# Attention: one reduce instruction for the row maxima of both heads of a pair

## The chip, the core and the metric

The kernel runs on one core of one Trainium2 chip. The metric is the device time of one execution in microseconds, as a median over several. The engines are named as in the profile: PE (TensorE, with its weight loads as PEld), DVE (VectorE), ACT (ScalarE), POOL (GpSimd) and SP (SyncE, here the issuer of DMAs).

## What is computed

Input x has 2 sequences of 2048 tokens with 256 features. Layer 0 adds a state-space scan and a product with sign weights. Layer 1 adds two attentions, each followed by its output product, and a mixture of 8 experts (top 2). The change lies in the two attentions alone:

```python
scores = einsum('bhqd,bhkd->bhqk', Q, K) * scale      # 16 heads of 16 features, causal
attn   = softmax(scores, axis=-1)                     # row maximum, exp, sum
out    = einsum('bhqk,bhkd->bqhd', attn, V)
```

The first has 16 heads of keys and values and position slopes added to the scores; the second has 4 heads of keys and values shared by 4 query heads each. The softmax subtracts each row's maximum, so the maxima of all rows over their causal keys are needed before the exponentials.

## The kernel before

The attention stage runs 16 steps (`STEPS`): 2 attentions, 2 sequences, 4 groups of 4 heads. The heads of a group are taken in pairs, `p` = 0 and 1; the two heads `j` = 0, 1 of a pair lie in the lower and the upper half of the partitions, so that PE can work at both at once. Query rows are cut into 4 blocks of 512 (`QB`).

Scores are made twice in a step. First come the maxima: for 128 queries and up to 512 keys (`WIDE`), PE writes queries x keys of both heads into two banks of PSUM (L1271, `max_pair` of the PE part, L1264), and on the diagonal adds masks with small bf16 products (L1256). DVE reduces each bank over its columns (L1444, `max_pair` of the DVE part, L1437) into `mx`. When all pieces of a block are there, L1451 reduces `mx` over the pieces, POOL splits the result into a high and a low part (L1215, L1217), PE turns it into rows (L1298), ACT copies them (L1394), and SP stores them by DMA as two more operand rows of the queries (L1163). Second come the scores proper, keys x queries, with these rows subtracting the maxima (L1286, `score_pair`), again two banks a pair; ACT takes the exponentials of each bank into `prob` (L1404), and PE multiplies the values with it, four heads side by side, into bank 7 (L1367). ACT copies a finished block out (L1424), PE turns it (L1376), and DVE divides by the row sums (L1465, L1469).

A step has 80 maxima pairs (`NMX`), 80 score pairs (`NSP`), 40 value products, 4 "rows" and 4 "turn" items. Their order is written out as a string (`ORDER`, and `FIRST_ORDER` for the first step, which has 130 maxima pairs since maxima run 50 pairs ahead, `LEAD`). All engines walk through the same list, each in order.

Banks 0 to 6 form a ring (`RING` = 7). `slot_table` (L1002) deals slots in the order of the list: two for a maxima or score pair, one for "rows" and "turn". A pair with slot number u sits in banks u mod 7 and (u + 1) mod 7, so it can wrap from bank 6 to bank 0. Before PE writes slots u and u + 1 it waits in `free_slots` (L1301) until slots u - 7 and u - 6 are free: for each kind of work it finds the newest item held there and waits once for its count. For maxima the semaphore is `s_md`, and each single reduce adds one to it, so there are 160 counts a step. For scores it is `s_ex`, one count for each exponential.

Of the kernel before, what the change touches and what calls it, by code (L numbers as in the profile page):

```python
# [6 lines left out]
ALU = mybir.AluOpType  # L7
ACT = mybir.ActivationFunctionType
AX = mybir.AxisListType
# [920 lines left out]
NQB = L // QB  # L930
KT = L // P
WIDE = 512
RING = 7
# [23 lines left out]
NSP, NMX = len(SCORES), len(MAXES)  # L957
# [44 lines left out]
def slot_table(work):  # L1002

    at, held = {}, []
    for what, n in work:
        if what in ("max", "score"):
            at[what, n] = len(held)
            held += [(what, 2 * n), (what, 2 * n + 1)]
        elif what in ("turn", "rows"):
            at[what, n] = len(held)  # L1010
            held.append((what, n))
    return at, held


def attention(nc, A, M):
# [4 lines left out]
    with ExitStack() as ctx:  # L1020
        def sb(name, shape, dt=F32):
            return ctx.enter_context(nc.sbuf_tensor(name, shape, dt))

        def sem(name):
            return nc.alloc_semaphore(name)

        ps, ident = M["ps"], M["ident"]
# [5 lines left out]
        mx = sb("a_mx", [P, 2, PAIRS, KT, L // WIDE])  # L1033
# [15 lines left out]
        s_md = sem("att_max_tile_reduced")  # L1049
# [21 lines left out]
        NSC = 2 * NSP  # L1071
        EX0, PV0, OE0, TT0, TE0, RT0, RE0, MP0, TOP0, MD0, HI0 = 16, NPB // GH, 1, 2, NQB, 1, NQB, 1, NQB, 512, 2
# [7 lines left out]
        def slot_sem(t):  # L1080

            return t if t < 2 else 2 + (t - 2) % 3
# [162 lines left out]
        def _(pe):  # L1245
# [55 lines left out]
            def free_slots(t, held, first, count):  # L1301

                last = {}
                for u in range(first - RING, first - RING + count):
                    past = u < 0
                    if past and t == 0:
                        continue
                    before = FIRST_HELD if t == 1 else HELD
                    what, n = before[u] if past else held[u]
                    while what == "pad":  # L1310
                        u -= RING
                        what, n = before[u]
                    back = {"max": 2 * NMX, "score": NSC, "turn": NQB, "rows": NQB}[what] if past else 0
                    last[what] = max(last.get(what, -1000), n + 1 - back)
                if "max" in last:
                    pe.wait_ge(s_md, t * (2 * NMX) + (last["max"] + MD0))
                if "turn" in last:
                    pe.wait_ge(s_te, t * NQB + (last["turn"] + TE0))
                if "rows" in last:
                    pe.wait_ge(s_re, t * NQB + (last["rows"] + RE0))  # L1320
                if "score" in last:
                    pe.wait_ge(s_ex, t * NSC + (last["score"] + EX0))

            pe.wait_ge(s_q[0], NFIRST)
            def step(t):
                o = t % 3
                work = work_of(t)
                slot_of, held = slot_table(work)
                for what, n in work:
                    if what != "value":  # L1330
                        u = slot_of[what, n]
                        outs = [ps[(u + j) % RING] for j in range(2)]
                    if what == "rows" and t == 0 and n == 0:
                        keep_going(pe, M, ps_o, 10)
                    if what == "max":
                        if t == 0 and n == KEYED[0]:
                            pe.wait_ge(s_k[0], NFK)
                        if t == 0 and n == KEYED[1]:
                            pe.wait_ge(s_k[1], NFK)
                        if n == NMX:  # L1340

                            pe.wait_ge(s_q[slot_sem(t + 1)], filled(t + 1) * NL)
                        free_slots(t, held, u, 2)
                        max_pair(t + n // NMX, n, outs)
                    elif what == "rows":
                        free_slots(t, held, u, 1)
                        turn_rows(t, n, u % RING)
                    elif what == "score":
                        qb, kt, p = SCORES[n % NSP]
                        if kt == 0 and p == 0:  # L1350

                            pe.wait_ge(s_mr[qb], (t + n // NSP + 1) * NMR)
                        free_slots(t, held, u, 2)
                        score_pair(t + n // NSP, n, outs)
                    elif what == "value":
                        qb, kt, _ = SCORES[n * PAIRS]
                        c0 = columns(qb, kt)
                        if n == 0:
                            pe.wait_ge(s_v[slot_sem(t)], filled(t) * 16)
                        if kt == 0:  # L1360

                            pe.wait_ge(s_oe, t * NQB + (qb + OE0))

                        pe.wait_ge(s_ex, t * NSC + (n * GH + GH + EX0))
                        for h in range(GH):
                            hk = 0 if t >= NGB else h
                            ins = pe.matmul(ps_o[VW * h:VW * h + VW, c0:QB], v_op[o][:, kt, hk * VW:hk * VW + VW],  # L1367
                                            prob[:, (n * GH + h) % NPB, c0:QB], start=(kt == 0),
                                            stop=(kt == 4 * qb + 3))
                        ins.then_inc(s_pv, 1)  # L1370
                    else:

                        free_slots(t, held, u, 1)
                        pe.wait_ge(s_oe, t * NQB + (n + 1 + OE0))
                        for j in range(4):
                            ins = pe.transpose(outs[0][:, j * P:(j + 1) * P],  # L1376
                                               o_sb[n % 2][:, j * P:(j + 1) * P], ident[:, :])
                        ins.then_inc(s_tt, 1)
# [50 lines left out]
        @block.vector  # L1429
        def _(dve):  # L1430
            v = nc.vector
            ch = Chain(dve, s_dve)
            dve.sem_inc(s_te, TE0)
            dve.sem_inc(s_md, MD0)
            dve.sem_inc(s_top, TOP0)

            def max_pair(t, n, banks):  # L1437
                qb, p, qt, k0, w = MAXES[n % NMX]
                if n % NMX == 0 or MAXES[n % NMX - 1][0] != qb:

                    dve.wait_ge(s_top, t * NQB + (n // NMX * NQB + qb - NQB + 1 + TOP0))
                dve.wait_ge(s_mt, t * NMX + (n + 1))
                for j in range(2):
                    v.tensor_reduce(mx[:, j, p, qt, k0 // WIDE:k0 // WIDE + 1], ps[banks[j]][:, 0:w], AX.X,  # L1444
                                    ALU.max).then_inc(s_md, 1)
                if n % NMX == LAST_MAX[qb]:
                    block = n // NMX * NQB + qb

                    dve.wait_ge(s_mp, t * NQB + (block + MP0))
                    dve.wait_ge(s_md, t * (2 * NMX) + (2 * (n + 1) + MD0))  # L1450
                    v.tensor_reduce(row_top[:, :, :], mx[:, :, :, 4 * qb:4 * (qb + 1), 0:qb + 1].rearrange(  # L1451
                        "p j h k c -> p (j h) k c"), AX.X, ALU.max).then_inc(s_top, 1)

            def step(t):
                work = work_of(t)
                slot_of = slot_table(work)[0]
                for what, n in work:
                    if what == "max":
                        max_pair(t, n, [(slot_of[what, n] + j) % RING for j in range(2)])
                    elif what == "turn":  # L1460
                        turned = ps[slot_of[what, n] % RING].rearrange("p (j h c) -> p j h c", j=4, h=GH)
                        dve.wait_ge(s_te, t * NQB + (n + TE0))
                        dve.wait_ge(s_tt, t * NQB + (n + 1 + TT0))

                        ch.did(v.reciprocal(rec[:, :, :], turned[:, :, :, HD]))  # L1465
                        ch.settle()

                        dve.wait_ge(s_os[n % 2], t * (NQB // 2 * 16) + (n // 2 * 16 + 16))
                        v.tensor_tensor(o_row[n % 2][:, :, :].rearrange("p j (h c) -> p j h c", h=GH),  # L1469
                                        turned[:, :, :, 0:HD],  # L1470
                                        rec[:, :, :].unsqueeze(3).to_broadcast([P, 4, GH, HD]), ALU.mult
                                        ).then_inc(s_te, 1)

            for t in range(STEPS):
                step(t)
# [884 lines left out]
```

## Time and profile before

| | us |
|---|---|
| median of 3 runs (lowest, highest) | 2559.83 (2559.28, 2562.41) |
| span of the profiled execution, first to last instruction | 2553.9 |
| its own time: the span and what lies around it, by the median | 2559.83 - 2553.9 = 5.9 around the span |
| attention stage in the profiled execution | 369.6 to 1972.3 |
| DVE busy, whole span | 1919.1 (75%) |
| PE busy, whole span | 2345.1 (92%) |
| L1444, the reduces | x2560, 1378.0 busy |

Busy is the time in which an engine had at least one instruction under way; instructions on one engine overlap a little, so the sum of their durations is more than the busy time. The idle time before an instruction is put down to the event that ended it. The mean granted clock of TensorE is given beside a stretch, 1.00 being 2.4 GHz.

### The profile page before, as it was taken

What the parts mean: (1) busy time and instruction counts of PE and PEld (TensorE: products, weight loads), DVE (VectorE), ACT (ScalarE), POOL (GpSimd) and SP (SyncE); (2) the same over time, 40 slices, a digit from 0 to 9 for tenths busy, and PEclk for the clock granted to TensorE, in tenths of its full rate; (3) what the DMA queues carried; (4) which work ended last, traced back from release to release, by engine and by line L of the source; (5) the groups of instructions that cost most, each with busy time, mean ns of one, the idle gap of its engine ahead of it and who ended that gap; (6) DMA issues with size and microseconds to landing.
All of it is one profiled execution on the core that took longest, in us unless ns stands there. A gap on an engine that the chain in (4) does not pass through costs nothing. (4 is left out here: it accounts for less than half of the span.)

```text
span 2553.9 us, 53242 instructions
## 1 busy us (share of the span) xinstructions
PE 2345.1 (92%) x18418; PEld 1285.1 (50%) x18419; DVE 1919.1 (75%) x4030; ACT 1519.8 (60%) x3292; POOL 583.1 (23%) x845
## 2 busy tenths in 40 slices
PE   3599988999999999999999999999999873999997
PEld 2355554444444444444444444444443662788886
DVE  7777659999999998998998999999992573333332
ACT  2133314777778778777787787777778561222221
POOL 5412002121111111111111111111000266432223
PEclk8799997999999999999999999999999996999999
DMA  4267775453343443322322322322121894344443
GB/s 157 77 194 217 209 182 91 72 110 76 67 85 76 71 79 70 62 51 54 63 56 46 71 54 48 66 54 52 31 79 37 290 299 173 68 75 76 77 74 70
DMA packets 168303, 246.56 MB, mean 97 GB/s; under 512 B 52392, under 2 KB 125240, under 8 KB 162244
## 3 DMA queue, kind: packets, MB, share of 16 engines
q0 software_dynamic: 38304, 112.51, 23.8%
q1 hardware_dynamic: 124740, 120.83, 16.1%
q10 hardware_dynamic: 5044, 10.32, 1.3%
q8 instruction: 139, 2.28, 0.4%
q14 instruction: 76, 0.62, 0.1%
HBM read 120.19 MB, written 122.36 MB: 95 GB/s over the span
## 5 line engine op out<-in xcount | busy, mean ns | idle before, releaser
L1444 DVE TENSOR_REDUCE a_mx<-banks 128x1 f32<-128x512 f32 (+3 forms) x2560 | 1378.0, 602 | 127.6 <-PE banks L1271 60.1
L1404 ACT ACTIVATE a_p<-banks 128x512 f32<-128x512 f32 (+3 forms) x2560 | 1177.9, 541 | 332.7 <-PE banks L1286 202.2
L1367 PE MATMUL banks<-a_p,a_v 128*32 128x512 f32 (+3 forms) x5120 | 599.3, 543 | 0.9 <-ACT a_p L1404 0.5
L1271 PE MATMUL banks<-a_k,a_q 48*128 48x512 f32 (+7 forms) x1600 | 340.7, 429 | 9.7 <-ACT a_p L1404 2.6
L1286 PE MATMUL banks<-a_q,a_k 50*128 50x512 f32 (+7 forms) x1600 | 332.2, 426 | 11.6 <-DVE a_mx L1444 4.4
L1271 PEld LDWEIGHTS banks<-a_k,a_q 52*128 52x128 f32 (+1 forms) x1600 | 154.6, 184 | 207.2 <-DVE a_mx L1444 164.5
L1286 PEld LDWEIGHTS banks<-a_q,a_k 54*128 54x128 f32 (+1 forms) x1600 | 152.3, 184 | 201.1 <-DVE a_mx L1444 145.3
L2136 ACT ACTIVATE e_hT<-banks 128x256 fp32r<-128x256 f32 x72 | 27.6, 383 | 308.7 <-PE banks L2062 279.0
L1271 PE MATMUL banks<-a_k,q 48*128 48x512 f32 (+7 forms) x896 | 192.0, 433 | 8.5 <-DMA a_k<-aug_rows 2.6
L2075 PE MATMUL banks<-w,e_hT 128*128 x576 | 184.1, 421 | 12.5 <-DVE e_hT L2176 11.6
L1286 PE MATMUL banks<-q,a_k 50*128 50x512 f32 (+7 forms) x896 | 186.8, 429 | 6.9 <-ACT a_p L1404 2.9
L2176 DVE TENSOR_TENSOR e_hT<-banks,e_hT 128x256 fp32r<-128x256 f32 x72 | 30.6, 424 | 192.7 <-ACT e_hT L2136 192.7
L2042 POOL DMA_INDIRECT out_rows<-e_y,e_token x72 | 111.6, 1550 | 250.9 <-DVE e_y L2196 173.1
L1367 PEld LDWEIGHTS banks<-a_p,a_v 128*32 128x32 f32 x5120 | 102.9, 108 | 113.8 <-issue 62.8
L1271 PEld LDWEIGHTS banks<-a_k,q 48*128 48x128 f32 (+1 forms) x896 | 87.8, 187 | 117.0 <-DVE a_mx L1444 91.6
L1286 PEld LDWEIGHTS banks<-q,a_k 50*128 50x128 f32 (+1 forms) x896 | 84.8, 185 | 122.9 <-DVE a_mx L1444 77.4
L2094 PE MATMUL banks<-w,e_gT 128*128 x576 | 136.5, 380 | 1.5 <-DVE e_y L2196 1.1
L2075 PEld LDWEIGHTS banks<-w,e_hT 128*128 128x128 f32 x576 | 109.6, 191 | 37.2 <-issue 13.8
L1256 PE MATMUL banks<-fill,before 64*128 64x64 bf16 x2048 | 124.6, 198 | 0.0
L1256 PE MATMUL banks<-fill,after 64*128 64x64 bf16 x2048 | 121.4, 197 | 0.0
L2094 PEld LDWEIGHTS banks<-w,e_gT 128*128 128x128 f32 x576 | 103.8, 190 | 13.5 <-issue 2.3
L1206 POOL DMA_DIRECT2D expert_rows<-a_zeros x132 | 98.6, 747 | 3.2 <-issue 3.2
(267 smaller groups left out, 2551.2 us busy)
## 6 DMA issues: line engine op xcount, KB each, us to landing
expert_rows<-a_zeros POOLq DMA_DIRECT2D x132, 258.0 KB, 5.4
a_k<-ka_parts POOLq DMA_DIRECT2D x42, 256.0 KB, 6.4
e_x<-expert_rows SPq DMA_DIRECT2D x72, 129.0 KB, 2.9
expert_rows<-e_y SPq DMA_DIRECT2D x72, 128.0 KB, 2.2
qa_parts<-m_part SPq DMA_DIRECT2D x16, 512.0 KB, 4.4
ka_parts<-m_part SPq DMA_DIRECT2D x16, 512.0 KB, 4.7
va_tiles<-m_va SPq DMA_DIRECT2D x8, 1024.0 KB, 4.5
qb_parts<-m_part SPq DMA_DIRECT2D x16, 512.0 KB, 4.8
```

The costliest lines, as they stand in the source:

```text
L1206: pool.dma_start(hs[:, i * FILL:(i + 1) * FILL, :], zeros[:, :, :]).then_inc(s_zs, 16)
L1256: ins = pe.matmul(outs[j][:, HALF * n:HALF * (n + 1)], steps[n][half, :], fill[half, :], start=False, stop=(n == 1))
L1271: ins = pe.matmul(outs[j][:, 0:w], q_op[o][part, p, qt * P:(qt + 1) * P], keys_of(r, k0)[part, kp, k0:k0 + w], start=True, stop=not diagonal)
L1286: ins = pe.matmul(outs[j][:, c0:QB], keys_of(r, kt * P)[part, kp, kt * P:(kt + 1) * P], q_op[o][part, p, qb * QB + c0:(qb + 1) * QB], star ...
L1367: ins = pe.matmul(ps_o[VW * h:VW * h + VW, c0:QB], v_op[o][:, kt, hk * VW:hk * VW + VW], prob[:, (n * GH + h) % NPB, c0:QB], start=(kt == ...
L1404: nc.scalar.activation(prob[:, (2 * n + j) % NPB, c0:QB], ps[(slot + j) % RING][:, c0:QB], ACT.Exp, scale=SCALE).then_inc(s_ex, 1)
L1444: v.tensor_reduce(mx[:, j, p, qt, k0 // WIDE:k0 // WIDE + 1], ps[banks[j]][:, 0:w], AX.X, ALU.max).then_inc(s_md, 1)
L2042: pool.indirect_dma_start(out=out, out_offset=bass.IndirectOffsetOnAxis(ap=token[n % R][:, :], axis=0), in_=y[n % R][:, :], in_offset=None ...
L2075: ins = pe.matmul(bank[:, :], hT[c][s][:, k, :], of[:, ds(at, 1), part * FFN:(part + 1) * FFN].rearrange("p o m -> p (o m)"), start=(k == ...
L2094: ins = pe.matmul(ps_y[:, 0:D], gT[s][:, f, :], w2[:, ds(e * FT + f, 1), :].rearrange("p o m -> p (o m)"), start=(f == 0), stop=(f == FT - 1))
L2136: nc.scalar.activation(hT[0][s][:, :, :].rearrange("p k t -> p (k t)"), ps_h[:, 0:D], ACT.Copy).then_inc(s_hi, 1)
L2176: v.tensor_tensor(hT[1][s][:, :, :].rearrange("p k t -> p (k t)"), ps_h[:, 0:D], high, ALU.subtract).then_inc(s_hT, 1)
```

## The change

Where the two banks of a maxima pair are neighbours, DVE reduces them with one instruction that reads both banks (2 x w columns) and writes two maxima. Where the pair wraps from bank 6 to bank 0, two instructions stay, and the banks are taken in the order 0, 6 by PE and by DVE. The semaphore `s_md` is raised once a pair, behind the last instruction of the pair, and `slot_table` counts both slots of a maxima pair under the pair's own number, so PE waits for whole pairs. The order strings are the same.

```diff
--- before.py
+++ after.py
@@ -1003,13 +1003,21 @@
 
     at, held = {}, []
     for what, n in work:
-        if what in ("max", "score"):
+        if what == "max":
+            at[what, n] = len(held)
+            held += [(what, n), (what, n)]
+        elif what == "score":
             at[what, n] = len(held)
             held += [(what, 2 * n), (what, 2 * n + 1)]
         elif what in ("turn", "rows"):
             at[what, n] = len(held)
             held.append((what, n))
     return at, held
+
+
+def pair_slots(u):
+
+    return sorted(((u + j) % RING for j in range(2)))
 
 
 def attention(nc, A, M):
@@ -1310,10 +1318,10 @@
                     while what == "pad":
                         u -= RING
                         what, n = before[u]
-                    back = {"max": 2 * NMX, "score": NSC, "turn": NQB, "rows": NQB}[what] if past else 0
+                    back = {"max": NMX, "score": NSC, "turn": NQB, "rows": NQB}[what] if past else 0
                     last[what] = max(last.get(what, -1000), n + 1 - back)
                 if "max" in last:
-                    pe.wait_ge(s_md, t * (2 * NMX) + (last["max"] + MD0))
+                    pe.wait_ge(s_md, t * NMX + (last["max"] + MD0))
                 if "turn" in last:
                     pe.wait_ge(s_te, t * NQB + (last["turn"] + TE0))
                 if "rows" in last:
@@ -1333,6 +1341,7 @@
                     if what == "rows" and t == 0 and n == 0:
                         keep_going(pe, M, ps_o, 10)
                     if what == "max":
+                        outs = [ps[slot] for slot in pair_slots(u)]
                         if t == 0 and n == KEYED[0]:
                             pe.wait_ge(s_k[0], NFK)
                         if t == 0 and n == KEYED[1]:
@@ -1434,20 +1443,25 @@
             dve.sem_inc(s_md, MD0)
             dve.sem_inc(s_top, TOP0)
 
-            def max_pair(t, n, banks):
+            def max_pair(t, n, slots):
                 qb, p, qt, k0, w = MAXES[n % NMX]
                 if n % NMX == 0 or MAXES[n % NMX - 1][0] != qb:
 
                     dve.wait_ge(s_top, t * NQB + (n // NMX * NQB + qb - NQB + 1 + TOP0))
                 dve.wait_ge(s_mt, t * NMX + (n + 1))
-                for j in range(2):
-                    v.tensor_reduce(mx[:, j, p, qt, k0 // WIDE:k0 // WIDE + 1], ps[banks[j]][:, 0:w], AX.X,
-                                    ALU.max).then_inc(s_md, 1)
+                low, high = slots
+                if high == low + 1:
+                    ins = v.tensor_reduce(mx[:, :, p, qt, k0 // WIDE], M["banks"][:, low:high + 1, 0:w], AX.X, ALU.max)
+                else:
+                    for j in range(2):
+                        ins = v.tensor_reduce(mx[:, j, p, qt, k0 // WIDE:k0 // WIDE + 1], ps[slots[j]][:, 0:w], AX.X,
+                                              ALU.max)
+                ins.then_inc(s_md, 1)
                 if n % NMX == LAST_MAX[qb]:
                     block = n // NMX * NQB + qb
 
                     dve.wait_ge(s_mp, t * NQB + (block + MP0))
-                    dve.wait_ge(s_md, t * (2 * NMX) + (2 * (n + 1) + MD0))
+                    dve.wait_ge(s_md, t * NMX + (n + 1 + MD0))
                     v.tensor_reduce(row_top[:, :, :], mx[:, :, :, 4 * qb:4 * (qb + 1), 0:qb + 1].rearrange(
                         "p j h k c -> p (j h) k c"), AX.X, ALU.max).then_inc(s_top, 1)
 
@@ -1456,7 +1470,7 @@
                 slot_of = slot_table(work)[0]
                 for what, n in work:
                     if what == "max":
-                        max_pair(t, n, [(slot_of[what, n] + j) % RING for j in range(2)])
+                        max_pair(t, n, pair_slots(slot_of[what, n]))
                     elif what == "turn":
                         turned = ps[slot_of[what, n] % RING].rearrange("p (j h c) -> p j h c", j=4, h=GH)
                         dve.wait_ge(s_te, t * NQB + (n + TE0))
```

## Rows read from the trace of the kernel before

**Rows 1.** The page: span; busy us, share and instructions of each engine

```profile
span 2553.9 us, 53242 instructions
PE 2345.1 (92%) x18418; PEld 1285.1 (50%) x18419; DVE 1919.1 (75%) x4030; ACT 1519.8 (60%) x3292; POOL 583.1 (23%) x845
```

**Rows 2.** Windows: first step, 14 equal steps, last step; busy us (instructions), clock

```profile
core 0: us, PE busy (x) PEld busy (x) DVE busy (x) ACT busy (x) POOL busy (x), PEclk, DMA share, GB/s
369.60:522.40 152.80, 138.40 (x1188) 66.56 (x1188) 138.98 (x273) 85.25 (x181) 30.68 (x63) 0.89 0.53 88
522.40:1893.00 1370.60, 1341.39 (x12993) 613.09 (x12992) 1249.83 (x2409) 1083.45 (x2352) 231.26 (x449) 1.00 0.33 63
1893.00:1972.30 79.30, 76.12 (x691) 30.14 (x690) 36.64 (x69) 69.72 (x158) 4.02 (x8) 1.00 0.24 68
```

**Rows 3.** Waits, eleven steps 717.7 to 1795.3: us, times, longest

```profile
PEld banks L1271 <- DVE a_mx L1444: 181.9, 384, 0.8
...
PEld banks L1286 <- DVE a_mx L1444: 159.7, 281, 1.1
...
DVE a_mx L1444 <- PE banks L1271: 41.0, 113, 0.9
DVE a_mx L1444 <- PE banks L1256: 36.0, 98, 0.7
```

**Rows 4.** Timeline, two places: start us, us, instruction, idle before and releaser

```profile
750.77 0.69 DVE L1444 TENSOR_REDUCE a_mx<-banks 128x1 f32<-128x512 f32 x1
...
751.38 0.68 DVE L1444 TENSOR_REDUCE a_mx<-banks 128x1 f32<-128x512 f32 x1
751.52 0.18 PEld L1286 LDWEIGHTS banks<-q,a_k 54*128 54x128 f32 x2 [0.24 <-DVE a_mx L1444]
...
1790.94 1.29 DVE L1444 TENSOR_REDUCE a_mx<-banks 128x1 f32<-128x512 f32 x2
...
1791.68 0.18 PEld L1286 LDWEIGHTS banks<-a_q,a_k 50*128 50x128 f32 x2 [0.18 <-DVE a_mx L1444]
```

**Rows 5.** Lines by form, DVE, one step 913.3 to 1011.3: count, busy us, mean ns

```profile
L1444 DVE TENSOR_REDUCE a_mx<-banks 128x1 f32<-128x512 f32 x112 | 70.3, 683 | 5.4 <-PE banks L1271 3.8 <-PE banks L1256 1.0
L1444 DVE TENSOR_REDUCE a_mx<-banks 128x1 f32<-128x384 f32 x16 | 8.1, 548 | 0.7 <-PE banks L1256 0.7
L1444 DVE TENSOR_REDUCE a_mx<-banks 128x1 f32<-128x256 f32 x16 | 6.0, 417 | 0.3 <-PE banks L1256 0.2
L1444 DVE TENSOR_REDUCE a_mx<-banks 128x1 f32<-128x128 f32 x16 | 3.9, 283 | 1.2 <-PE banks L1256 1.2
...
L1451 DVE TENSOR_REDUCE a_rowtop<-a_mx 128x16 f32<-128x64 f32 x1 | 0.2, 219 | 0.1
```

**Rows 6.** Timeline of DVE: two heads of one pair, back to back

```profile
1008.47 1.28 DVE L1444 TENSOR_REDUCE a_mx<-banks 128x1 f32<-128x512 f32 x2
```

**Rows 7.** Timeline: a burst on DVE, and a maxima pair behind a value product on PE

```profile
723.34 13.14 DVE L1444 TENSOR_REDUCE a_mx<-banks 128x1 f32<-128x512 f32 x23
...
730.89 1.07 PE L1367 MATMUL banks<-a_p,a_v 128*32 128x512 f32 x8
...
731.89 0.49 PE L1271 MATMUL banks<-a_k,q 52*128 52x512 f32 x2
```

**Rows 8.** The page: the chain that ended last, by line

```profile
PE banks L2075 7%; PE banks L2094 5%; PE banks L2086 1%; PE banks L2062 1%; DMA out_rows<-e_y,e_token 0%; DMA e_last<-expert_rows,places 0%; DMA expert_rows<-e_y 0%; POOL t_w13low L2028 0%; DVE e_y L2196 0%; SPq L1995 0%; DVE e_sum L2221 0%; DVE e_sum L2223 0%; POOLq L1951 0%; DVE e_hT L2176 0%; POOL e_last L2035 0%
```

**Rows 9.** Timeline, two places where PE started before its pair was reduced

```profile
720.45 0.28 DVE L1444 TENSOR_REDUCE a_mx<-banks 128x1 f32<-128x128 f32 x1
...
720.47 0.38 PEld L1286 LDWEIGHTS banks<-q,a_k 54*128 54x128 f32 x4 [0.18 <-issue]
...
1792.45 1.28 DVE L1444 TENSOR_REDUCE a_mx<-banks 128x1 f32<-128x512 f32 x2
...
1793.45 0.19 PEld L1286 LDWEIGHTS banks<-a_q,a_k 50*128 50x128 f32 x2
```

## The prediction

> **What bounds the kernel now.** I read the busy shares first, then the stretches, then the waits, then single microseconds of the timeline. The attention stage runs from 369.6 to 1972.3 us, 1602.7 of the 2553.9 us [rows 1, 2]. Its 16 steps are one pattern: a long first step, 14 equal ones of 97.9 us (1370.6 / 14), and a short last one with hardly a maximum in it [rows 2]. In the equal steps DVE is busy 91% (1249.83 of 1370.6) and PE 98%, at a granted clock of 1.00, which is the 2.4 GHz level. PE's busy share is flattering: a weight load of a maxima or score pair waited for DVE's L1444 in 384 + 281 cases over eleven steps, 341.6 us in all, 31 us a step [rows 3]. DVE itself waited for PE 77 us at L1444 over the same eleven steps, 7 a step [rows 3]. So neither engine is simply the bound. DVE is nearly full, and PE asks for banks about as fast as DVE frees them: the stage is a loop through a ring of seven banks.
>
> The reader should see that loop in the ring's arithmetic. A pair placed at slots u and u+1 reuses slots u-7 and u-6. Seven is odd, so in a run of pairs one of these is the *second* head of the fourth pair back, the other the *first* head of the third pair back. The newest thing PE must wait for is then one head, not a pair. Counting the order string of a normal step, 136 of the 160 maxima and score pairs reuse some maxima slot, and for 78 of them (38 maxima, 40 scores) the newest maxima slot is a first head. PE uses this: head 0 is reduced from 750.77 to 751.46, head 1 from 751.38 to 752.06, and PE loads weights at 751.52, 0.06 us behind head 0 and 0.54 ahead of head 1; near the end of the stretch, the pair 1790.94 to 1792.23 has PE following at 1791.68 [rows 4].
>
> **Part 1, fewer instructions: a gain on DVE.** A reduce lasts 683, 548, 417 and 283 ns at 512, 384, 256 and 128 columns [rows 5]: (683 - 283) / 384 = 1.042 ns a column. Two at 512 columns back to back take 1.28 us [rows 6], so the second begins 0.597 after the first; of that 0.533 are columns and 0.064 is the fixed part that overlaps nothing. One instruction over 1024 columns should take 0.683 + 0.533 = 1.216 us and let the next begin after 1.131, against 1.194 for two: 0.064 us saved per merged pair at any width. Where the pair starts in bank 6 it wraps to 0 and is not merged: 14 of a step's 80. Merged are 66 in each of 14 steps, 112 of 130 in the first, 23 of 30 in the last, together 1059, so DVE is relieved of 68 us. Two results instead of one are no cost that shows: the 16-result reduce of 64 columns takes 219 ns [rows 5], less than a one-result reduce of 128. Bounds for one merge: 0 if the fixed part comes back per bank, 0.150 (0.683 - 0.533) if all that is not columns went. I take 0.064, the row for back-to-back work.
>
> The Trainium skill, Perfetto Trace Analysis, Optimizing Scalar/DVE Operations, gives VectorE on PSUM an overhead of about 125 ns per instruction and says grouping helps a saturated engine; by that figure DVE would be relieved of 1059 x 0.125 = 132 us, an estimate from that page. The 0.597 us in this trace contradicts it.
>
> **Part 2, one signal per pair: a loss on PE.** The semaphore now counts pairs. Each of the 78 placements a step that needed a first head now waits for the whole pair. Merged, a pair's end comes 0.533 us later than head 0's did at 512 columns, 0.13 at 128; a wrapped pair keeps two instructions but signals after the second, 0.60 later. Behind the waiting PE instruction stand, in order, the next pairs and value products, so ACT and then DVE are fed later. Placements that needed a second head gain 0.064. What hides this today is DVE's backlog: from 723.34 DVE reduces 23 heads without a gap while PE waits [rows 7], and a later start of PE costs nothing as long as its pair is there when DVE gets to it. If that cover is gone, it costs in full.
>
> **Which of both lies on the path.** The printed chain of waits shows only what follows attention [rows 8], so I walked back through the trace's start and end times from the last maxima over the eleven steps from 717.7 to 1795.3, at every instruction to whatever ended last. The walk crosses 258 whole pairs on DVE (23.5 a step) and leaves DVE for PE 69 times (6.3 a step) behind a first head; the first and the last of the 69 are in [rows 4]. Priced anew, that one path is a lower estimate: gain 23.5 x 66/80 x 0.064 = 1.2 us a step, loss 6.3 x 0.533 = 3.3, net +2.1. A second term: 171 more placements on the walk (15.5 a step, 0.23 us each on average, 3.6 a step) were bound by PE's own queue and now come before their pair's end; of the last, the pair is reduced from 1792.45 to 1793.73 and PE loads at 1793.45, and of the first the reduce ends at 720.73 with PE's loads running from 720.47 to 720.85 [rows 9]. Such slips within one visit to PE don't add, the longest decides, and DVE's backlog eats some. Between none and all of the 3.6 I take half, 1.8. Together +3.9 us a step, x 14 = +55. The first step has 11 such exits and 63 pairs (52 merged) on the walk: 11 x 0.533 - 52 x 0.064 = +2.5. The last has next to no maxima: 0. Sum +58.
>
> No DMA is added; POOL's and SP's loads are paced by PE's scores and stay hidden. The exchange of the two banks of a wrapped pair changes who holds which bank, not when. Everything behind 1972.3 moves by the same amount. The profiled execution's span is 2553.9; against the median of 2559.83 some 5.9 us lie around it, unchanged: 2559.8 + 58 = **2618 us**.
>
> The same section of the Trainium skill (Perfetto Trace Analysis, Optimizing Scalar/DVE Operations) says that where Vector is not saturated but makes others idle, *breaking up* instructions may let work complete sooner. That is this change read backwards, and the 31 us a step of PE behind L1444 agree with it.
>
> **Rivals.**
> *Coarser release* (forecast), 0.68: 2618, own range 2575 to 2680 (2.1 to 5.7 us a step with the two terms at their ends gives 2592 to 2642, widened for a lost planning fit).
> *DVE's relief wins*, 0.20: place, the bursts of 10 us and more in L1444; if the stage follows DVE's work, all 68 us come back, 2492, and with half of it 2526. For it: 91% busy. Against: it decides only if PE, released late, still has the next maxima pair ready when DVE ends; a maxima pair takes 0.49 us from load to end and a value product ahead of it 1.00 (730.89 to 731.89), against the merged pair's 1.13 on DVE [rows 7], so there is little room.
> *They cancel*, 0.06: 2560, if the exits on the walk shrink to about two a step (1.2 / 0.533).
> *Every slip adds*, 0.06: 665 / 11 = 60 waits a step, 78/136 of them behind a first head, 35 x 0.45 us = 16 less 4: +12 a step, +168, 2728. Against: DVE's backlog.
> The range of 2540 to 2680 leaves out most of the second and the fourth, about 0.2. No change means within 0.2%, 5 us, about what a measurement of this kernel can tell: faster 0.20, same 0.05, slower 0.75.
>
> **What would show it.** Merged reduces of 2x512 at 1.216 us and DVE's count of L1444 at 2560 - 1059 = 1501; L1444 busy down by about 68. Equal steps of about 101.8 us. PE's wait for L1444 up from 31 to 35 or more a step, DVE's idle before L1444 up from 7 to some 15. Wrong if steps are at or below 97.9: then PE's later releases were hidden. If a merged reduce lasts much over 1.22 us, part 1 is wrong.

## The result, and the profile after

The changed kernel takes 2682.04 us (median of 4 runs, 2680.33 to 2682.70) against 2560.82 for the one before beside it: a ratio of 1.047, 95% interval 1.0455 to 1.0484. That is 121 us more. Forecast were 58 more, 2618 us, with 2680 as the upper end of the range. The sign and the kind of cause were right; the size was half, because the forecast priced only one path through the old trace (see below).

The page, with the span and each engine's busy time, count of instructions and share, to be held against [rows 1]: DVE has 1059 instructions less and is busy 54 us less, over a span 126 us longer. The span grew more than the median time because the profiled execution of the kernel before was a quick one: in every execution recorded with its span the time lies 1.8 to 1.9 us above the span (here 2681.68 - 2679.8), so the 5.9 us in the table of the kernel before are these 1.9 and some 4 us of difference between executions.

```profile
span 2679.8 us, 52183 instructions
...
PE 2382.6 (89%) x18418; PEld 1278.8 (48%) x18419; DVE 1865.0 (70%) x2971; ACT 1537.7 (57%) x3292; POOL 582.6 (22%) x845
```

The stage by the same three stretches as [rows 2], from windows of the changed kernel's trace:

```profile
core 0: us, PE busy (x) PEld busy (x) DVE busy (x) ACT busy (x) POOL busy (x), PEclk, DMA share, GB/s
369.60:533.80 164.20, 147.51 (x1186) 70.40 (x1186) 134.75 (x162) 85.63 (x181) 31.21 (x62) 0.82 0.50 84
533.80:2014.00 1480.20, 1367.96 (x12993) 603.03 (x12992) 1203.46 (x1484) 1100.92 (x2353) 231.41 (x449) 0.99 0.30 58
2014.00:2096.00 82.00, 76.68 (x691) 29.77 (x690) 35.54 (x46) 69.84 (x156) 3.28 (x6) 1.00 0.21 63
```

The first step grows from 152.8 to 164.2 us, the 14 equal ones from 1370.6 to 1480.2 (from 97.9 to 105.7 each), the last from 79.3 to 82.0. These 123.7 us are nearly all of it; 2 us come later. Two single steps of the same kernel, by the same columns:

```profile
638.80:744.00 105.20, 96.89 (x929) 42.69 (x928) 85.97 (x106) 78.56 (x169) 17.06 (x33) 1.00 0.38 70
955.50:1062.80 107.30, 99.49 (x931) 43.97 (x930) 85.99 (x106) 78.92 (x169) 17.01 (x33) 0.97 0.37 69
```

The first is one of nine that last 104.9 to 105.2 us at clock 1.00. The second lasts 2.1 us more at a mean of 0.97; five of the 14 steps hold such a stretch of 3 to 7 us at the lower level, 1.2 GHz. Before, the clock stayed at 1.00 through all 14. So of the 109.6 us about 100 (14 x 7.1) are the new order of waits, and 10 are the clock.

The reduces by form over eleven steps (744.0 to 1909.1), the answer to [rows 5]: a merged pair at 2 x 512 columns takes 1.221 us where 1.216 was worked out, and 0.950, 0.690 and 0.421 for the narrower ones.

```profile
L1454 DVE TENSOR_REDUCE a_mx<-banks 128x2 f32<-128x1024 f32 x495 | 598.0, 1221 | 127.5 <-PE banks L1279 95.4 <-PE banks L1264 29.3
L1457 DVE TENSOR_REDUCE a_mx<-banks 128x1 f32<-128x512 f32 x242 | 155.3, 683 | 14.1 <-PE banks L1279 13.6
L1454 DVE TENSOR_REDUCE a_mx<-banks 128x2 f32<-128x768 f32 x77 | 73.1, 950 | 0.5
L1454 DVE TENSOR_REDUCE a_mx<-banks 128x2 f32<-128x512 f32 x88 | 60.7, 690 | 16.3 <-PE banks L1264 16.1
L1454 DVE TENSOR_REDUCE a_mx<-banks 128x2 f32<-128x256 f32 x66 | 27.8, 421 | 28.6 <-PE banks L1264 28.6
```

The waits over the same eleven steps, the answer to [rows 3]:

```profile
PEld banks L1294 <- DVE a_mx L1454: 150.7, 232, 1.1
PEld banks L1279 <- DVE a_mx L1454: 140.1, 252, 0.9
...
DVE a_mx L1454 <- PE banks L1279: 95.4, 165, 2.5
...
DVE a_mx L1454 <- PE banks L1264: 74.0, 110, 1.3
PEld banks L1294 <- DVE a_mx L1457: 67.3, 99, 1.4
...
DVE a_mx L1457 <- PE banks L1279: 13.6, 33, 0.8
DVE a_mx L1457 <- PE banks L1264: 13.3, 22, 0.9
PEld banks L1279 <- DVE a_mx L1457: 11.7, 22, 0.8
```

PE's weight loads waited 370 us for L1454 and L1457 in place of 342, and DVE waited 196 us for PE (17.8 us a step) in place of 77 (7.0). DVE's part is the signature forecast ("some 15"): the engine that got less to do starves more. PE's part is 33.6 us a step, up from 31 but short of the 35 or more that were forecast. The single place below, from the timeline, shows the handover, to be held against [rows 4]: the merged reduce ends at 750.15 and PE loads at 750.20, into slots of which the newest, by the slot table, is the first head of that pair. With two reduces and two signals this head would have been free near 749.61 (748.92 + 0.69, an estimate).

```profile
748.92 1.23 DVE L1454 TENSOR_REDUCE a_mx<-banks 128x2 f32<-128x1024 f32 x1
...
750.06 1.28 DVE L1457 TENSOR_REDUCE a_mx<-banks 128x1 f32<-128x512 f32 x2
750.20 0.19 PEld L1294 LDWEIGHTS banks<-q,a_k 54*128 54x128 f32 x2 [0.56 <-DVE a_mx L1454]
...
751.27 0.19 PEld L1279 LDWEIGHTS banks<-a_k,q 52*128 52x128 f32 x2 [0.41 <-issue]
```

### The profile page after: what moved, and what is told of

It is laid out like the page before. It is cut to its first block and busy times, and to the rows that moved or that the text cites. A ratio compares the mean times of both kernels' runs of the same rounds, so it can differ in the third digit from the quotient of the medians.

```text
span 2679.8 us, 52183 instructions
## 1 busy us (share of the span) xinstructions
PE 2382.6 (89%) x18418; PEld 1278.8 (48%) x18419; DVE 1865.0 (70%) x2971; ACT 1537.7 (57%) x3292; POOL 582.6 (22%) x845
## 5 line engine op out<-in xcount | busy, mean ns | idle before, releaser
L1454 DVE TENSOR_REDUCE a_mx<-banks 128x2 f32<-128x1024 f32 (+3 forms) x1059 | 1088.6, 1056 | 251.2 <-PE banks L1279 139.6
L1376 PE MATMUL banks<-a_p,a_v 128*32 128x512 f32 (+3 forms) x5120 | 606.5, 549 | 0.9 <-ACT a_p L1413 0.5
L1279 PE MATMUL banks<-a_k,a_q 48*128 48x512 f32 (+7 forms) x1600 | 342.3, 430 | 24.7 <-DVE a_mx L1454 17.1
L1457 DVE TENSOR_REDUCE a_mx<-banks 128x1 f32<-128x512 f32 (+3 forms) x442 | 253.8, 616 | 40.6 <-PE banks L1279 20.9
L1376 PEld LDWEIGHTS banks<-a_p,a_v 128*32 128x32 f32 x5120 | 103.8, 109 | 122.1 <-ACT a_p L1413 53.4
L2108 PEld LDWEIGHTS banks<-w,e_gT 128*128 128x128 f32 x576 | 103.8, 190 | 12.9 <-issue 1.8
```

Of the source, the lines that this page charges most:

```text
L1279: ins = pe.matmul(outs[j][:, 0:w], q_op[o][part, p, qt * P:(qt + 1) * P], keys_of(r, k0)[part, kp, k0:k0 + w], start=True, stop=not diagonal)
L1454: ins = v.tensor_reduce(mx[:, :, p, qt, k0 // WIDE], M["banks"][:, low:high + 1, 0:w], AX.X, ALU.max)
L1457: ins = v.tensor_reduce(mx[:, j, p, qt, k0 // WIDE:k0 // WIDE + 1], ps[slots[j]][:, 0:w], AX.X, ALU.max)
L2108: ins = pe.matmul(ps_y[:, 0:D], gT[s][:, f, :], w2[:, ds(e * FT + f, 1), :].rearrange("p o m -> p (o m)"), start=(f == 0), stop=(f == FT - 1))
```

## The experiments

All are variants of the kernel before. In e1 to e7 the count still goes by heads; a table says for each pair how it signals. A step is measured from one start to the next of the same score pair, and steps are compared where the clock stays at 1.00.

**e1: late signal, nothing merged.**

```diff
-                for j in range(2):
-                    v.tensor_reduce(mx[:, j, p, qt, ...], ps[banks[j]][:, 0:w], AX.X,
-                                    ALU.max).then_inc(s_md, 1)
+                how = mode_of(t, n)      # e1: "late" for all
...
+                        ins = v.tensor_reduce(mx[:, j, p, qt, ...], ps[banks[j]][:, 0:w], AX.X, ALU.max)
+                        if how != "late":
+                            ins.then_inc(s_md, 1)
+                    if how == "late":
+                        ins.then_inc(s_md, 2)
```

> The kernel before, with its two reduces per pair, but the first head raises no signal and the second raises two: PE always learns of a whole pair, as in the changed kernel, and no instruction is merged. Theory R (the late release alone makes the loss, and the merging gives a little of it back): slower than the changed kernel by the fixed part that the merging saved, 0.064 us for each merged pair that the way back through the changed kernel's trace crosses (some 30 of a step's 66, 1.9 us a step), so 2682 + 27 = about 2710 us, at most 2682 + 68 = 2750. Rival M (reading two banks in one instruction is itself the cost, for example because PE's writes and DVE's reads meet): the late signal costs what I forecast, 58 plus the 68 x 0.3 that the merging no longer returns, about 2635 us, and the changed kernel's other 60 us are missing here.

Measured: 2714.97 us, ratio 1.0619 (1.0603 to 1.0636). The windows of its 14 equal steps, and of one step at clock 1.00:

```profile
542.20:2055.60 1513.40, 1379.57 (x12993) 600.63 (x12992) 1252.73 (x2408) 1104.16 (x2353) 231.46 (x449) 0.99 0.29 57
542.20:649.50 107.30, 97.60 (x929) 42.54 (x928) 89.36 (x172) 79.22 (x169) 16.98 (x33) 1.00 0.42 82
```

Theory R's number to within 5 us. The late signal alone costs all that the change costs and more; the changed kernel is 33 us faster than e1 (38 by the two ratios). In a step at clock 1.00 the late signal costs 9.4 us (107.3 - 97.9), and merging returns 2.3 of it (107.3 against 105.0). What one merge saves on DVE can be read from the pages: DVE is busy 1922.9 us in e1 and 1865.0 in the changed kernel, 57.9 us over 1059 merged pairs or 0.055 us each; 2.3 us are 42 of a step's 66 merged pairs at that price. The changed kernel also exchanges the banks of a wrapped pair, which e1 does not; the two were not tried apart. Rival M is out.

**e2: the six pairs that the way back left by their first head.** `mode_of` is "late" for pairs 77, 99, 104, 124, 126 and 127 of the equal steps, "each" for the rest.

> Two reduces per pair as before; in the 14 equal steps only the six pairs (77, 99, 104, 124, 126, 127 of the step's numbering) behind whose first head the way back through the trace of before leaves DVE for PE signal both heads after the second. My own pricing of one path says 6 x 0.53 to 0.60 = 3.2 to 3.4 us a step, x 14 = +45 to +48, about 2607 us. Rival (each of these delays is caught by the next backlog of DVE): under 1 us a step, below 2575.

Measured: 2621.84 us, ratio 1.0251 (1.0235 to 1.0267), +66 us and so above both numbers. Two neighbouring steps show where the rest lies:

```profile
629.70:730.50 100.80, 95.72 (x929) 43.55 (x929) 89.17 (x172) 76.91 (x167) 17.05 (x33) 1.00 0.40 73
730.50:834.30 103.80, 98.70 (x929) 44.91 (x928) 89.21 (x172) 78.39 (x171) 17.01 (x33) 0.97 0.38 71
```

At clock 1.00 the step lasts 100.8 us (100.8 to 101.4 in seven of the 14, +3.1), which is the price worked out. The other seven hold stretches at 1.2 GHz and last 3 us longer, one of them 8, and these make most of the remainder. The cause of these dips wasn't tried by itself. A few microseconds more lie in the first step, where no pair is treated otherwise than before: 156.1 us with 47.8 of them at the lower clock, against 152.8 with 34.1.

**e3: the 74 others.** The same table the other way round.

> The counterpart: in the 14 equal steps the 74 pairs that are not these six signal late, the six signal each head at once. If pricing the one path of before were enough, only half of its 15.5 further placements would tell, 1.8 us a step, +25, about 2586 us. Theory W (the way moves: with so many releases late, other loops between DVE and PE become the longest, and which six were on it before means little): most of the loss of the late release stays, at least 5 us a step, +70 to +110, 2630 to 2670 us.

Measured: 2654.54 us, ratio 1.0389 (1.0373 to 1.0405). Its 14 equal steps, with 104.7 us each at clock 1.00:

```profile
519.80:1985.70 1465.90, 1371.68 (x12993) 598.98 (x12992) 1252.30 (x2409) 1102.43 (x2353) 231.85 (x450) 1.00 0.31 59
```

The pairs by which the old way did *not* leave DVE cost 6.8 us a step, twice what the six cost. Theory W holds.

**e4: merging where there was room.** 23 pairs of a step "merge" (one instruction over both banks, raising the count by two), from the second step on.

```diff
+SPARE = (50, 52, 55, 60, 64, 69, 71, 74, 76, 78, 79, 85, 91, 94, 96, 103, 106, 108, 109, 111, 115, 119, 121)
...
+                if how == "merge" and banks[1] == banks[0] + 1:
+                    v.tensor_reduce(mx[:, :, p, qt, k0 // WIDE], M["banks"][:, banks[0]:banks[1] + 1, 0:w], AX.X,
+                                    ALU.max).then_inc(s_md, 2)
```

> The kernel before with the merged instruction only for 23 of a step's 80 pairs (from the second step on): those whose first head's bank PE in the trace of before never took up before the whole pair would have been reduced. The merged instruction raises the count by two, PE's waits are as before. Theory R: nothing is released too late, DVE is relieved of 23 x 0.064 = 1.5 us a step; the share of pairs that the way back crosses is 23.5 of 80, so 0.4 us a step or 6 us in all are gained, at most 22: 2539 to 2556 us. Rival M (the two-bank instruction costs by itself): slower than before, 2570 or more.

Measured: 2558.07 us, ratio 1.0006 (0.9997 to 1.0015): no change. The groups of DVE's reduces over the whole run show the 333 merged ones beside 1894 single ones:

```profile
L1457 DVE TENSOR_REDUCE a_mx<-banks 128x1 f32<-128x512 f32 (+3 forms) x1894 | 1034.6, 603 | 71.9 <-PE banks L1264 34.9 <-PE banks L1279 29.1 <-DVE a_rowtop L1468 0.2
L1453 DVE TENSOR_REDUCE a_mx<-banks 128x2 f32<-128x1024 f32 (+2 forms) x333 | 349.1, 1052 | 72.8 <-PE banks L1279 41.4 <-PE banks L1264 26.6 <-issue 0.3
```

The expected gain of 6 us is not there, and neither is rival M's loss. DVE is relieved as meant: it is busy 1900.7 us in place of 1919.1, 0.055 us for each of the 333 merged pairs. That this relief buys nothing where DVE was not the one waited for is the reading that fits; which engine was waited for at these places wasn't looked at one by one.

**e5 and e6: the rest, parted.** e5 makes 16 pairs late (51, 65, 67, 75, 82, 83, 84, 86, 87, 95, 97, 100, 102, 112, 125, 128), e6 the 58 that are neither in e2 nor in e5.

> Two reduces per pair; in the 14 equal steps only 16 pairs signal late: those whose first head's bank was taken up early by a placement that lies on the way back through the trace of before, though that way did not leave DVE there. These carry the second term of my sum, which I put at 1.8 us a step and at most 3.6. If that term was right in itself, the equal steps measure 99.2 to 101.5 us against 97.9 where the granted clock stays at 1.00. Theory W (ways through other pairs carry the loss) has no other number here, but must then show it in the next run.

> The 58 remaining pairs of an equal step signal late, and the 22 on or beside the way back signal each head. A forecast from the one way through before has nothing to pay here: 97.9 us a step, 2556 us, within 5. Theory W: these pairs carry what is left of the 6.8 us a step that the 74 pairs cost together: 3 to 5 us a step, 2600 to 2625 us.

Measured: e5 2602.33 us, ratio 1.0170 (1.0153 to 1.0187); e6 2624.07 us, ratio 1.0241 (1.0224 to 1.0258). One step at clock 1.00 of each:

```profile
520.60:621.50 100.90, 97.32 (x930) 43.29 (x930) 89.48 (x173) 77.67 (x168) 17.69 (x34) 1.00 0.45 91
```

```profile
520.20:622.20 102.00, 96.50 (x930) 42.99 (x928) 89.54 (x173) 78.72 (x169) 17.62 (x34) 1.00 0.45 91
```

e5 costs 3.1 us a step on average at clock 1.00, within the bounds of the second term but nearer to all of it than to half. e6 costs 4.3, where the old way alone says nothing is to be paid. The trace of the kernel before, read pair by pair with the slot table, shows what the one way left out: at 21 pairs of an equal step PE loads 0.05 us after the first head is reduced, so it was waiting for just that head. Six of these 21 are the exits priced in e2; 12 are among e6's 58 pairs. Another 23 of the 58 are the pairs with room that e4 merged. Each of the three sets by itself is slower than before, and their sum, 3.1 + 3.1 + 4.3 = 10.5, is a little over the 9.4 of all together.

**e7: the changed kernel's treatment in the first step alone**, "merge" or, at the wrap, "late" for t = 0.

> The changed kernel's treatment (merged where neighbours, one signal a pair) in the first step alone. My sum had +2.5 us for it. The trace of the changed kernel has the first step 11.5 us longer, with 58 us of it at the lower granted clock against 34. If that belongs to the step itself: 2556 + 8 to 12 = 2564 to 2568 us, with a first step of 161 to 165 us and more of it at the lower clock. If it was chance of that execution: within 4 us of before.

Measured: 2569.67 us, ratio 1.0034 (1.0019 to 1.0048), +8 us. The first step and the 14 equal ones of its profile:

```profile
368.00:533.10 165.10, 145.50 (x1186) 68.85 (x1186) 135.00 (x162) 85.59 (x181) 31.36 (x62) 0.84 0.50 84
533.10:1903.70 1370.60, 1341.65 (x12995) 612.69 (x12994) 1250.04 (x2408) 1083.80 (x2352) 231.64 (x449) 1.00 0.32 63
```

The first step lasts 165.1 us as in the changed kernel, at a clock of 0.84 against 0.89 before [rows 2]; the equal steps are those of before to the tenth. It belongs to the step. How much of it is clock and how much waits wasn't parted by a run. An estimate comes from e2's first step, where 13.7 us more at the lower clock went with 3.3 us more time: e7 has 17.1 us more at the lower clock (51.2 against 34.1), which at that rate is 4 of its 12 us.

**e8 and e9: the other direction.** e8 hands each head of a maxima pair over by itself, off the diagonal; e9 does so too, and for score pairs and ACT as well. The diff is e8's, shortened.

```diff
-                        free_slots(t, held, u, 2)
...
+                if diagonal:
+                    free(0, 2)
                 for j in range(2):
+                    if not diagonal:
+                        free(j, 1)
                     ... the product of head j
+                    if not diagonal:
+                        ins.then_inc(s_mt, 1)
...
+                    if j == 0 or not diagonal:
+                        dve.wait_ge(s_mt, t * (2 * NMX) + (2 * n + (2 if diagonal else j + 1)))
```

> The opposite of the change: off the diagonal PE takes up the bank of head 0 and signals it to DVE alone, then that of head 1, each as soon as it is free. Theory R (the loop between DVE and PE through the ring sets the stage, and a finer handover shortens it): the way back through before returns from PE to DVE 11.5 times a step; where it does so off the diagonal, DVE can start up to a head's wait earlier. 1 to 3 us a step, 2515 to 2542 us. Rival (DVE's work or PE's work bounds the stage in before): no change, or slower by some us since the two heads' products no longer run side by side.

> Both kinds of pairs handed over head by head off the diagonal: maxima to DVE as in e8, scores to ACT too. The way back through before passes from ACT to PE 12.5 times a step, so an earlier start of ACT's first head could count for as much as DVE's did: e8 gained 4 us in all, and this should gain 4 to 12 us, 2545 to 2555 us beside a before of about 2558. Rival: e8's gain came from the first step alone and ACT has slack; then this stays with e8 within 2 us, or loses by the scores' products no longer running side by side.

Measured: e8 2557.04 us beside 2561.34, ratio 0.9982 (0.9972 to 0.9991); e9 2546.68 beside 2558.17, ratio 0.9961 (0.9946 to 0.9975). The 14 equal steps of e8, then of e9:

```profile
520.10:1888.80 1368.70, 1340.89 (x12995) 617.60 (x12994) 1248.01 (x2409) 1083.77 (x2352) 232.35 (x451) 1.00 0.33 63
```

```profile
519.30:1882.20 1362.90, 1348.04 (x12993) 634.51 (x12992) 1247.93 (x2409) 1080.15 (x2352) 232.28 (x449) 1.00 0.33 63
```

e8 gains 0.1 us an equal step and 2 us in the first. That is far from the 1 to 3 us a step that I expected, and at the edge of what can be told. e9 gains 0.55 a step (97.35 against 97.9) and is 10 to 11 us faster than before, the fastest of all kernels here, though its seven executions reach from 2543 to 2557 us. The sign agrees with the loop. The size says that starting both sides head by head is worth much less here than a later *end* costs; how much of the gain is lost again because the two heads' products no longer start together wasn't parted.

**e10: an even ring.** `RING = 6` in place of 7, one bank then idle.

> The kernel before with a ring of six banks instead of seven (bank 7 of the eight then idle, the value products in bank 6), each head signalled by itself. With an even ring a pair mostly takes up the two banks of one earlier pair, the third one back, so PE waits for whole pairs even though each head is signalled. Theory R: that is the late release by another road. It costs what e1 costs, 9 us an equal step (+140 in all, 2700 us), and more, since the scores' pairs lose their first heads as well: 2700 to 2760 us. Rival (what e1 lost is the delayed signal and not the bank's return): clearly less than e1, under 2660.

Measured: 2810.78 us, ratio 1.0984 (1.0968 to 1.1000), 50 us above the upper end of theory R. Its waits over the whole run; in the kernel before the same four, in this order, were 232.5, 263.2, 22.9 and 41.0 us:

```profile
PEld banks L1286 <- DVE a_mx L1444: 276.1, 430, 1.7
PEld banks L1271 <- DVE a_mx L1444: 200.3, 332, 1.7
...
PEld banks L1271 <- ACT a_p L1404: 170.3, 349, 1.7
PEld banks L1286 <- ACT a_p L1404: 142.4, 236, 1.1
```

PE's loads wait for DVE 476 us, no more than the 496 before, and for ACT 313 us, five times as long. So the loss shows up behind ACT as much as behind DVE, where I had expected e1's picture. Its equal steps at clock 1.00 last 111.2 to 112.2 us, 13 to 14 more than before where e1's last 9.4 more. By the slot table no pair of it has a first head as the newest slot, as meant. This kernel also has one bank less, so it doesn't part the parity of the ring from the bank; what an even ring costs by itself stays open.

## Why the prediction was off, step by step

- *The price of one merge*, 0.064 us: a little high, 0.055 by e1 against the changed kernel and by e4. The reduce lasts 1.221 (1.216 worked out). DVE's busy time was to fall by about 68 us and fell by 54 (1919.1 to 1865.0): 10 of the missing 14 are this price. The other 4 are there without any merging, for e1's DVE is busy 3.8 us longer than before: an instruction's last 0.09 us overlap the next one where both stand back to back, and with more gaps between them less is overlapped. The instructions fell to 1501 as said.
- *The late signal is on the path*: right. e1, which has it and no merging, loses 9.4 us a step; e4, which merges and releases nothing too late, loses nothing.
- *The six exits, 3.3 us a step*: right, 3.1 in e2 at clock 1.00.
- *"Such slips within one visit to PE don't add, the longest decides, and DVE's backlog eats some ... I take half, 1.8"*: mis-sized; e5 measures 3.1.
- *"Which of both lies on the path"*: the step that failed. I priced anew the one way through the trace of before and took what lay off it as free but for that term. The 58 pairs off it cost 4.3 us a step alone (e6), and 12 of them are places where PE already stood waiting for a first head. The waits moved with it: over eleven steps DVE waits for PE 330 times in the changed kernel and 211 times in the one before. That other loops through these places became the longest is the reading of this, and it was not followed loop by loop.
- *The one way itself* is no firm thing: walked by the profile's own rule (a release counts only if it came after the printed end of the instruction before), it returns from PE to DVE 5.5 times a step through the trace of before, where my walk had 11.5, so the choice hangs on how near ties are decided. One path gave a lower estimate (+32 in all), which I had said, but the rest was then taken too small.
- *The rival in which every slip adds*, 2728 us with a chance of 0.06, was nearer to the measured 2682 than my 2618; its 16 us a step for the late signal are too many, as my 5.1 (3.3 and 1.8) are too few: 9.4 measured.
- *Merging's gain, 1.2 us a step*: too small, 2.3 (e1 against the changed kernel). That DVE is on the longest way at more pairs once the signals are late would explain it, and isn't shown.
- *The first step, +2.5*: wrong, +11.4 in the profile, and +8 by e7's runs. The late signal alone makes it longer still, 173.8 us in e1.
- *The last step, 0*: +2.7. The late signal brings it by itself: e1's last step is 82.8 us against 79.3.
- *The 5.9 us around the span*: 1.9 in every execution. It cancels in the forecast, which adds to the median.
- *The clock*: not priced. Ten microseconds in the equal steps and a part of the first step are lost at 1.2 GHz.

In sums: equal steps 14 x (9.4 - 2.3) = 99 us where I had 14 x 3.9 = 55, clock 10 where I had none, first step 11 for 2.5, last 3 for 0: 123, in profiles whose spans differ by 126.

The Trainium skill, Perfetto Trace Analysis, Optimizing Scalar/DVE Operations, says that breaking up instructions may let work complete sooner where Scalar or Vector aren't saturated but make other engines idle. The grouping here went the way that this suggests, with +121 us; but e1 loses more without grouping anything, so what counts is when the buffer is handed back. No run here breaks up an instruction: e9, 10 to 11 us faster, has the reduces of before and breaks up the handover. The overhead of about 125 ns per instruction for VectorE on PSUM, from the same section, is not what a merge saves here; the runs show 0.055 us.

## What to carry to other kernels

Before joining two instructions that free buffers, ask who takes up the first one's buffer and when; the fixed part saved (0.055 us) is to be held against a buffer that comes back up to 0.53 us later, at every place where that buffer is the newest waited for. The product of delay and places is only an upper bound: there are 78 such places in a step, and the step lost 9.4 us. When many places have less slack than the new delay, the critical path of the old trace prices only a part (here 3.1 of 9.4 us a step): it is better to list how long after the first buffer's release each place takes it up, and to look first at those that wait for it (21 a step here, six of them on the path). As a way to forecast this wasn't tried. A ring of seven banks lets the producer of pairs follow half a pair behind its consumer, and a signal per pair gives that away.

## What I had not expected of the hardware

The granted clock, at 1.00 through all equal steps before, fell to 1.2 GHz for 3 to 14 us at a time in the changed kernel (3 to 7), e1, e2, e5, e6 and e10; e2, the kernel with the least waiting added besides e5, has it in seven of 14 steps and e3, which is slower, in none. The other executions agree: e2's four have a mean clock of 0.955 to 0.962 over the whole kernel, e3's four 0.965 to 0.968. So the dips don't follow the amount of waiting, and what sets them stays open. A dip of 7 us makes a step some 3 us longer (e2: 103.8 against 100.8).
